# Deformable convolution and attention on one core: hand-placed order tables per engine, and token turns moved to the row-sum banks

## The reference

```python
x = x + deform_conv(group_norm(x))        # 3x3 taps, each with its own learned shift, bilinear
t = tokens(x)                             # 8 x 1024 x 64
t = t + attention(ln(t))                  # one head of 64, causal, 1024 queries and keys
t = t + experts(ln(t))                    # 32 experts, each takes its 8 best tokens per image
```

## Time and profile before

| | us |
|---|---|
| median of three executions | 601.82 (600.0 to 602.16) |
| the profiled execution | 599.73 |
| its span, first to last instruction | 597.9 |
| busy in the span: PE, PEld, DVE, ACT, POOL | 471.5, 322.1, 307.3, 277.9, 142.2 |
| mean granted clock of TensorE, as a share of 2.4 GHz | 0.852 |

### The profile page before, as it was taken

One profiled execution on the slowest core, in us unless ns is written; L12 is line 12 of the kernel. 1 busy time (PEld: TensorE's weight loads), 2 busy tenths in 40 slices (PEclk: granted clock), 3 DMA queues, 4 the chain that ended last, 5 costly groups with the idle time before them and its releaser, 6 DMA issues. The chain is left out here.

```text
span 597.9 us, 13359 instructions
## 1 busy us (share of the span) xinstructions
PE 471.5 (79%) x5651; PEld 322.1 (54%) x5651; DVE 307.3 (51%) x446; ACT 277.9 (46%) x457; POOL 142.2 (24%) x113
## 2 busy tenths in 40 slices
PE   2407877899899988998899889989988967825585
PEld 1105654656565665665566566655755643423364
DVE  3225656486647564756674657465655444223023
ACT  1223633575456555655666266636645523502210
POOL 4400034034023411342152305230223123031000
PEclk9957868999979988998999689969998965875577
DMA  9589697687356636654584458346540000005606
GB/s 235 103 184 218 165 224 190 141 197 180 85 139 161 156 90 159 156 133 124 148 208 106 99 123 210 99 123 164 139 100 2 1 0 1 1 2 114 203 2 141
DMA packets 31953, 75.10 MB, mean 126 GB/s; under 512 B 21581, under 2 KB 23437, under 8 KB 25549
## 3 DMA queue, kind: packets, MB, share of 16 engines
q1 hardware_dynamic: 27006, 72.16, 51.2%
q10 hardware_dynamic: 4880, 2.01, 1.3%
HBM read 65.04 MB, written 7.01 MB: 121 GB/s over the span
## 5 line engine op out<-in xcount | busy, mean ns | idle before, releaser
L701 DVE TENSOR_TENSOR wring<-stage 96x640 f32<-96x640 f32 x192 | 157.9, 851 | 110.8 <-ACT stage L560 104.3
L874 PE MATMUL psum<-wring,zring 96*64 96x160 f32 (+4 forms) x1728 | 150.8, 312 | 19.2 <-ACT wA L1147 17.1
L874 PEld LDWEIGHTS psum<-wring,zring 96*64 96x64 f32 x1728 | 118.7, 154 | 52.2 <-issue 33.1
L567 ACT ACTIVATE zring<-psum 96x768 f32<-96x768 f32 x64 | 51.5, 805 | 91.8 <-PE psum L841 91.8
L745 PE MATMUL psum<-keys,asked 64*128 64x128 f32 (+3 forms) x240 | 58.3, 522 | 27.0 <-DVE asked L663 16.2
L667 DVE TENSOR_REDUCE negmax<-psum 128x1 f32<-128x256 f32 (+3 forms) x64 | 52.6, 821 | 49.6 <-PE psum L751 49.0
L586 ACT ACTIVATE pT<-psum 128x512 f32<-128x512 f32 (+2 forms) x96 | 46.8, 488 | 67.3 <-PE psum L762 66.5
L841 PE MATMUL psum<-kern,img 64*32 64x192 f32 x1536 | 65.0, 373 | 9.4 <-ACT zring L567 4.1
L762 PE MATMUL psum<-const,prob 128*128 128x128 f32 x288 | 52.5, 294 | 8.5 <-ACT pT L586 6.2
L605 ACT ACTIVATE prob<-psum,negmax 128x256 f32<-128x256 f32 (+3 forms) x64 | 50.4, 788 | 10.3 <-DVE negmax L667 10.1
L254 POOL TENSOR_SCALAR gs<-gs 64x1 f32<-64x1 f32 x8 | 9.1, 1139 | 167.9 <-DVE gs L246 167.9
(11 more groups left out here) (120 smaller groups left out, 507.6 us busy)
## 6 DMA issues: line engine op xcount, KB each, us to landing
stage<-near SPq DMA_DIRECT2D x192, 288.0 KB, 4.9
w<-in_w SPq DMA_DIRECT2D x1, 2080.0 KB
tok<-in_x SPq DMA_DIRECT2D x8, 256.0 KB, 5.9
img<-img SPq DMA_DIRECT2D x8, 256.0 KB, 3.1
images<-img SPq DMA_DIRECT2D x8, 256.0 KB, 3.7
w<-in_w SPq DMA_DIRECT2D x1, 2048.0 KB
near<-tents SPq DMA_DIRECT2D x32, 45.0 KB
shifts<-offT SPq DMA_DIRECT2D x8, 128.0 KB, 5.0
```

The lines of the kernel that those rows point to most:

```text
L567: act.activation(zring[0:KX, q % ZRING].rearrange("p (s e) f -> p e s f", e=2), psum[0:KX, 0:2, 0:2 * K * C].rearrange("p e (s f) -> p e s ...
L701: dve.tensor_tensor(rows[:, ky, :, place], stage[0:KX, q % STG, ky, 1:, :], stage[0:KX, q % STG, ky, 0, :].unsqueeze(1).to_broadcast([KX, ...
L874: ins = pe.matmul(psum[C * e:C * e + C, 2 + half, (lo % 16) * W:(lo % 16 + n) * W], zring[0:KX, q % ZRING, i % 2 * 2 + e, ky * C:(ky + 1) ...
```

## The change

- The common grid of 36 steps goes. Each engine has its own table of places: `PE_TURN` (65 places), `ACT_TURN` (56), `DVE_TURN` (49); places above a table's length fall into the next turn. The helpers `stands` and `which` look a place up; `turn_tables` picks the table.
- Turns go from b = 0 to 8 instead of 9. In the last one image 7 follows the `_LAST` tables and what is left of image 6 the `_LATE` tables.
- Pairs stand two by two in places, and the masks are written as a step of their own ahead of the scores (`pe_mask`, start=True), the scores adding to them.
- Tokens, projections, tokens2 and logits use banks 0 and 1 in place of 4 and 5. All users of banks 0 and 1 wait through `take_shared` for the last user's evacuation. The scores no longer wait for the logits.
- Image 7's odd score blocks use banks 2 and 3, its odd chunks bank 1.
- The sum into the tokens (x2) is a step of its own, at the place behind share.

The arithmetic is the same. The rest of the diff replaces step numbers by table look-ups.

```diff
@@ the tables (their _LAST and _LATE forms are cut to PE's and DVE's) @@
-        AT_X, AT_RAW, AT_STATS, AT_GROUPS, AT_SCALES = 25, 26, 28, 30, 31
-        AT_OFF, AT_LEAVE, AT_DISTANCES, AT_TENT = 7, 8, 9, 10
-        AT_VALUES = [AT_PROBS[t + 1] + 3 + t // 4 for t in range(0, NT, 2)]
-        AT_OUT = AT_VALUES[-1] + 1
-        AT_SUM2, AT_SQUARES2 = AT_OUT + 3, AT_OUT + 5
-        AT_LN2, LOGITS_AFTER = NU + AT_SCORES[2] + 3, 2
+        PE_TURN = dict(
+            n=65,
+            pair=[8, 10, 14, 16, 23, 24, 26, 28, 33, 34, 38, 43, 49, 50, 56, 57],
+            z=[1, 12, 22, 29, 44, 48, 55, 61],
+            back=3,
+            lift=51,
+            groups=64,
+            offsets=17,
+            tokens=20,
+            query=25,
+            mask=[19, 30, 35, 41, 46, 53, 60, 70],
+            scores=[27, 31, 36, 42, 47, 54, 62, 71],
+            turned=[32, 40, 45, 52, 59, 63, 67, 69, 72, 76, 78, 80],
+            values=[58, 65, 74, 83],
+            out=86,
+            tokens2=102,
+            logits=104,)
+        PE_LAST = dict(
+            n=52,
+            back=2,
+            tokens=13,
+            query=14,
+            mask=[15, 16, 19, 23, 26, 31, 34, 38],
+            scores=[17, 18, 21, 24, 27, 32, 35, 39],
+            turned=[20, 28, 29, 33, 36, 37, 40, 41, 43, 44, 45, 46],
+            values=[30, 42, 47, 48],
+            out=49,
+            tokens2=50,
+            logits=51,)
+        PE_LATE = dict(
+            n=52,
+            mask=[-1, -1, -1, -1, -1, -1, -1, 3],
+            scores=[-1, -1, -1, -1, -1, -1, -1, 5],
+            turned=[-1, -1, -1, -1, -1, -1, 1, 4, 6, 7, 9, 10],
+            values=[-1, 0, 8, 11],
+            out=12,
+            tokens2=22,
+            logits=25,)
+        ACT_TURN = dict(
+            n=56,
+            z=[5, 13, 22, 32, 39, 42, 49, 52],
+            abs=[8, 15, 18, 24, 29, 45, 50, 53],
+            relu=[9, 16, 21, 28, 34, 47, 54, 55],
+            half=40,
+            rest=1,
+            raw=44,
+            leave=17,
+            tent=[23, 26],
+            keys=20,
+            query=25,
+            exp=[27, 30, 35, 38, 43, 48, 58, 66],
+            turned=[31, 37, 41, 46, 51, 56, 59, 60, 63, 67, 68, 70],
+            values=75,
+            keys2=89,
+            logits=92,
+            choice=6,)
...
+        DVE_TURN = dict(
+            n=49,
+            weights=[0, 5, 6, 7, 9, 11, 12, 13, 14, 19, 21, 24, 26, 27, 28, 31, 32, 33, 39, 40, 41, 45, 46, 47],
+            x1=2,
+            raw=35,
+            stats=37,
+            scales=42,
+            distances=15,
+            sum=3,
+            squares=8,
+            query=20,
+            max=[22, 25, 29, 30, 34, 36, 44, 53],
+            share=65,
+            x2=66,
+            sum2=67,
+            squares2=72,
+            choice=[1, 10, 38, 92, 97],)
+        DVE_LAST = dict(
+            n=26,
+            x1=2,
+            sum=3,
+            squares=4,
+            query=11,
+            max=[12, 14, 15, 16, 18, 19, 20, 21],
+            share=22,
+            x2=23,
+            sum2=24,
+            squares2=25,
+            choice=[0, 5, 6, 13, 17],)
+        DVE_LATE = dict(
+            n=26,
+            max=[-1, -1, -1, -1, -1, -1, -1, 1],
+            share=7,
+            x2=8,
+            sum2=9,
+            squares2=10,)
@@ banks @@
-            return 0 if alone(a) and t % 2 else 4
+            return 2 if alone(a) and t % 2 else 4
-            return 3 if alone(a) and n % 2 else 6
+            return 1 if alone(a) and n % 2 else 6
-                    ins = pe.matmul(psum[:, 4 + h, :], wA[C * h:C * h + C, :], keys[C * h:C * h + C, :],
+                    ins = pe.matmul(psum[:, h, :], wA[C * h:C * h + C, :], keys[C * h:C * h + C, :],
@@ who used banks 0 and 1 last @@
+        def take_shared(pe, user, i):
+            last, j = shared
+            if last == "z":
+                pe.wait_ge(f["z_sb"], j + 1)
+            if last == "lift":
+                pe.wait_ge(prep.s["raw_lo"], j + 1)
+                pe.wait_ge(prep.s["raw_hi"], j + 1)
...
+            if last == "query":
+                pe.wait_ge(s["q_sb"], ONE + j + 1)
+                pe.wait_ge(s["k_sb"], ONE + j + 1)
+            if last == "tokens2":
+                pe.wait_ge(s["lnT2"], ONE + j + 1)
+            if last == "logits":
+                pe.wait_ge(s["lg_sb"], ONE + j + 1)
+            shared[:] = [user, i]
@@ masks ahead of scores @@
+        def pe_mask(pe, a, t):
+            pe.wait_ge(s["ex"], ONE + a * NT + (max(t - 1, 0) if alone(a) else t))
+            if t == 1 and alone(a):
+                pe.wait_ge(s["x1"], ONE + a + 1)
+            bank, i, odd = score_bank(t, a), t // 2, t % 2
+            query = slice(i * P, (i + 1) * P)
+            if not odd:
+                pe.matmul(psum[:, bank + 1, query], exact[:, 0, :], exact[:, 2, :], start=True, stop=(t == 0),
+                          skip_group_check=True)
+            pe.matmul(psum[:, bank + odd, query], exact[:, 0, :], exact[:, 1, :], start=True, stop=False,
+                      skip_group_check=True)
-            if t == (LAST_AFTER_LOGITS if alone(a) else AFTER_LOGITS):
-                pe.wait_ge(s["lg_sb"], ONE + a)
@@ turns @@
-                for b in range(B + 2):
+                for b in range(B + 1):
                     pe_turn(pe, b)
```

More of the change, by code:

```diff
@@ new lines, in convolve_and_attend @@
+        ACT_LAST = dict(
+            n=39,
+            rest=0,
+            keys=12,
+            query=13,
+            exp=[14, 15, 18, 21, 23, 25, 28, 31],
+            turned=[17, 20, 22, 24, 26, 27, 29, 30, 32, 33, 34, 35],
+            values=36,
+            keys2=37,
+            logits=38,
+            choice=5,)
+        ACT_LATE = dict(
+            n=39,
+            exp=[-1, -1, -1, -1, -1, -1, 2, 7],
+            turned=[-1, -1, -1, -1, -1, 1, 3, 4, 6, 8, 9, 10],
+            values=11,
+            keys2=16,
+            logits=19,)
@@ new lines, in convolve_and_attend, with turn_tables @@
+        DVE_LAST = dict(
[17 more added lines that the diff above has]
+            squares2=10,)
+        def turn_tables(turn, last, late, b):
+            if b < B:
+                return turn, turn, turn["n"]
+            return last, late, 0
@@ L461, in mix_piece, with stands, which @@
+        def stands(at, name, n):
+            return at.get(name, -1) == n
+        def which(at, name, n):
+            return at[name].index(n) if n in at.get(name, ()) else None
         def mix_piece(pe, m, bank, done):
@@ L488, in alive @@
             return not isinstance(b, int) or 0 <= b < B
[L490 to L507, removed]
-            return None
         def logit_place(a):
@@ L637, in act_turn @@
                         prep.keep_raw(act, b + 2, 0)
-                    if n == AT_LEAVE and alive(b + 1):
+                    if stands(at, "leave", n) and alive(b + 1):
                         prep.leave(act, b + 1)
-                    for step in range(2):
-                        if n == AT_TENT + step and alive(b + 1):
-                            prep.tent(act, b + 1, step)
-                attention_steps(act, act_attention, b, n)
-                if b == B and n == AT_CHOICE[0] + 1:
+                    if which(at, "tent", n) is not None and alive(b + 1):
+                        prep.tent(act, b + 1, which(at, "tent", n))
@@ new lines, in pe_turn @@
+                    if which(at, "pair", n) is not None:
+                        conv_pair(pe, b, which(at, "pair", n), touched)
+                    g = which(at, "z", n)
+                    if g is not None and PIECES * b + g + 2 < NG4:
+                        take_shared(pe, "z", PIECES * b + g + 2)
+                        mix_rows(pe, PIECES * b + g + 2)
+                    if stands(at, "lift", n) and alive(b + 2):
+                        take_shared(pe, "lift", b + 2)
+                        prep.to_channels(pe, b + 2)
@@ new lines, in pe_turn @@
+                    if stands(at, "groups", n) and alive(b + 2):
+                        take_shared(pe, "groups", b + 2)
+                        prep.group_sums(pe, b + 2)
+                    if stands(at, "offsets", n) and alive(b + 1):
+                        take_shared(pe, "offsets", b + 1)
+                        prep.offsets(pe, b + 1)
+                    if stands(at, "offsets", n) and b == B - 1:
+                        take_shared(pe, "largest", 0)
+                        prep.largest_in_row(pe)
@@ L928, in fast_path_over @@
+                if stands(at, "back", n) and alive(b - 1):
+                    conv_back(pe, b - 1)
+                if alive(b - 2):
+                    pe_attention(pe, b - 2, n + past, late)
+                if alive(b - 1):
+                    pe_attention(pe, b - 1, n, at)
         def fast_path_over(eng):
```

240 lines of the change are left out of this document (105 added, 135 removed).

## The result

The changed kernel takes 534.26 us (median of 4, 530.36 to 535.99) beside 601.9 us (median of 4, 600.0 to 602.16) for the kernel before on the same chip: a ratio of 0.8873, 95% interval 0.8821 to 0.8925. Faster, as forecast, by 68 us where 56 were predicted; 534 lies in the range of 522 to 578.

The account below looks back on a forecast made before the run. It took TensorE (PE) to bound the kernel; full turns -40.7, turn 7 -5.8, turn 1 -2.4 and last images -7.0 sum to -55.9 us: 543.8 profiled, 546 as median, range 522 to 578, chance 0.65.

Parts of the forecast that it names:

- The bound: Five full turns: TensorE (PE) bounds; its work at full clock is 47.2 us a turn, less 0.4, of 57.4.
- the wait for asked: First scores waiting for DVE's copy of the projected queries: 16.2 us in 8 times, to fall under 5.
- The stall and its second price: First scores: the 2.57 us wait goes, and with it the slow clock following it, which costs as much as all idling.
- Rival A: Full turns: stall goes, clock falls all the same from other waits or thin products; turn 53.5, 571 us; chance 0.15.
- Idle and clock of the full turns: Full turns: 1.5 us idle and 1.0 for the clock a turn, making 49.3 us; five turns -40.7 us.
- Modes side by side: PE's tile-mode changes fall from 401 to 367 at 0.10 us each: 0.4 us a full turn, 3.4 in all.
- Rival D: Whole kernel: the change does only what its words say, products side by side; 3.4 us, 598 us; chance 0.04.
- Banks: Scores' 6.5 us of waits for logits go; handovers of banks 0 and 1 are covered, with 29 us of 48 used.
- Rival C: Banks 0 and 1 become the bound, 1.0 us a handover; full turn 61.5 us, about 625 us; chance 0.07.
- Turn 1, turn 7, turn 0: Short turns: turn 1 45.8 us (-2.4), turn 7 43.6 us (-5.8), turn 0 held by loads, 39.7 us (0).
- Last images: Up to the end of out: earlier first scores -2.2 us, own table -4.8, together -7.0, from 0 to -15.
- DMA share: Full turns: DMA's share rises from 0.58 to 0.68, short of the 0.89 of the first turn.

Follow-up runs that it names:

- experiment 2: Changed kernel with the Relu of the third piece behind both tents (ACT place 27 instead of 21): 594.51 us, ratio 1.0008.
- experiment 3: Changed kernel with the third piece's Relu at ACT's place 26: 570.27 us; or with DVE's copy of the queries at place 22 instead of 20: 547.57 us.
- experiment 7: Changed kernel with the squares of image 6's second LN later on DVE: place 12, 534.66 us; place 15 with a choice step moved too, 534.06 us.
- experiment 5: Changed kernel with the masks back behind the scores of their block: 538.42 us, ratio 0.9019.
- experiment 4: Changed kernel with tokens, projections and logits of the full turns back in banks 4 and 5, with the waits this needs: 566.07 us, ratio 0.9462.
- experiment 1: Kernel before with DVE's copy of the projected queries one step earlier: 603.45 us, ratio 1.0185.
- experiment 9: Kernel before with the copy of the queries one step earlier and share, sum into the tokens and second LN's sums 2 to 4 later: 609.64 us, ratio 1.0229.

## Why the prediction was right, and where it was off

**The bound.** Right: PE's work at the full clock bounds the full turns. The prediction had 46.8 us for it, and 47.4 was measured. The turns of 47.6 us on average lie below the 48 to 50 that it named as its sign, for the reasons below; its other signs came (clock 1.00 in them, the wait for asked at 3.8 us, low stretches only outside them).

**The stall and its second price.** Right, and the largest part. "The slow clock follows the stall" was the main assumption; experiments 2 and 3 show it. At one place, with all else equal:

| idle ahead of the first scores, us | full turn, us | low clock behind it, us |
|---|---|---|
| 0 (changed kernel) | 47.7 | 0 |
| 1.18 | 48.9 | 0 in the profiled execution |
| 1.82 | 49.5 to 56.2 | 0 to 17.1 |
| 2.78 | 57.9 | 17.1 |

The order of time foreseen around the scores came out step by step, at 4.6 us for 5.0. Rival A, that the clock falls for another reason, falls for the full turns: with the stall gone the clock holds, and with the stall alone put back it drops. In the last images experiment 7 shows a low stretch that no single long wait precedes.

**Idle and clock of the full turns.** This term of the sum was mis-sized. "I take 1.5" of idling was 0.16 on average (0.8 us in five turns), the 1.0 for "a clock that now and then still falls" was nothing, and work was 0.6 more. Together 47.6 for 49.3, so -49.3 instead of -40.7 us. The price of idling isn't smooth, and the estimate treated it as if it were: it put a middling idle time beside a middling clock loss. By the table, a stall of 1.2 us brought none of the low clock in the profiled execution, the same 1.82 us between none and 17.1 us of it, and 2.8 us the 17.1 in every full turn. Once every cover holds, both terms go to zero together.

The work came out 0.6 more because the prediction took off too much for the clock: it counted half the length of every low stretch as lost. Turns of one kernel that idle alike show less. In experiment 3 the turn with 3.4 us of low clock is 1.4 us longer than the one with none (50.9 for 49.5), and that with 13.7 us is 6.0 longer (55.5). In experiment 2 a turn is 10.2 us longer than in the changed kernel; 2.65 of it is more idling, which leaves 7.6 for 17.1 us. That is 0.41 to 0.44 of the length, and an estimate at 0.44 for the kernel before (some 51.7 us of low clock in its full turns) gives a loss of 22.7 us for the 25.8, or 0.6 more work a turn.

**Modes side by side.** Right in size as far as it was tried: 0.4 us a turn was priced for four changes, and experiment 5 has 0.43 for two of them and some idling. The Trainium skill, "TensorEngine Tiling (Array Packing)", section "Key Properties", says that a change of tiling mode drains TensorE; by that sentence the change costs something, and the 0.10 us a time of the earlier trace rows is what it is here. Rival D, that this is all the change does, falls: it is some 3 of 68 us by estimate (34 changes of 0.10), and experiment 2 loses nearly the whole gain with every one of these changes still saved.

**Banks.** The cover that the prediction counted (29 of 48 us) was enough, and PE loses nothing in take_shared. That the move is needed was underestimated. The prediction booked it as 6.5 us of waits for logits gone; experiment 4 puts it at some 30 us in this order of places, most of it by the clock, as in the new order the token turn would wait 1.9 us for banks 4 and 5. Rival C, a wait of 1 us a handover, doesn't appear: ACT is busy 163.9 of 237.9 us and follows. "PSUM Bottleneck" of the same page of the Trainium skill, which spoke for it, isn't borne out here either after the change. (The arithmetic of two rivals is off by 0.2: five turns of 53.5 us are -19.7 and five of 61.5 are +20.3. Nothing hangs on it.)

The parts aren't a sum. Without the Relu's place 60 us are lost, without the banks some 30, and the gain was 68. Each fault alone brings a stall or two, and one of 2.8 us a turn is enough for the low clock in every full turn; in the kernel before, mending one of several brought nothing (experiments 1 and 9). That was not in the prediction, which priced the old kernel's stall as if it could be taken out alone.

**Turn 1, turn 7, turn 0.** 46.3, 43.3 and 39.5 us for 45.8, 43.6 and 39.7. Right in size; in turn 1 two errors cancel. The wait for the first image's LN was kept at the 3.44 us of the earlier trace rows and fell to 1.16, and the clock was lower than assumed (0.86; 0.93 before). A low stretch of 10.2 us that lay at 76.3 to 86.5 us in the kernel before, in turn 0, now lies at 86.6 to 96.8, almost all of it in turn 1. It begins within the 3.64 us for which the turn back at 87.73 waits. Turn 0, at clock 0.89 instead of 0.78, takes 39.5 us for 39.7.

**Last images.** Mis-sized: -11.0 for -7.0 us, inside the bounds of 0 to -15. The squares waiting for POOL ahead of the copy came as foreseen. The scores started 19.6 us after the turn back, where the prediction had 19.0 (21.2 before). What it missed lies behind them: 24.2 us to the end of out, forecast 28.7, before 33.8. There PE idles 2.2 us, forecast 5, and at clock 0.86 the same working gives a clock loss of 3.4, forecast 5.5, as the clock is low for 6.8 us only. The own tables are 4.9 us of the 11.0.

**DMA share.** 0.68 was forecast for the full turns and 0.75 came, for two reasons: the turns got shorter still, and a piece takes longer to land (5.6 us, had 4.9). It never stands ahead of PE in the full turns.

## What to carry to other kernels

Where a stall of two to three microseconds stands ahead of every low stretch of TensorE's clock, price it with that stretch: here 2.8 us of idling a turn cost 10.2. Such a gain doesn't come in parts that add up, since the stall moves to the next late step when one instruction is moved, so lay out for each engine what stands between two products and check every cover before building. And look afterwards not at the sum of the edits but at which single place, put back, brings the stall again.

## What the runs showed of the hardware that was not expected

POOL got slower, with the same instructions. In the earlier trace rows the product of 64x1024 took 3784 ns and that of 128x512 1041 ns; in the changed kernel:

```profile
L258 POOL TENSOR_SCALAR img<-img,gs 64x1024 f32<-64x1024 f32 x8 | 44.1, 5513 | 0.9
L1338 POOL TENSOR_TENSOR norm_tmp<-tok,rn_small 128x512 f32<-128x512 f32 x8 | 11.2, 1397 | 66.4 <-DVE rn_small L1319 66.4
```

The traces show what goes with it. First the product in a full turn of the changed kernel, then the same one in experiment 2, where DVE stands idle beside it because its weights product waits for the late Relu:

```profile
202.23 1.52 POOL L1338 TENSOR_TENSOR norm_tmp<-tok,rn_small 128x512 f32<-128x512 f32 x1 [6.25 <-DVE rn_small L1319]
```

```profile
166.77 1.04 POOL L1338 TENSOR_TENSOR norm_tmp<-tok,rn_small 128x512 f32<-128x512 f32 x1 [6.25 <-DVE rn_small L1319]
```

With a weights product of DVE beside it (202.02, 0.82 us) it takes 1.52 us, with none 1.04, and so it is in each of the five full turns of both kernels. It goes the other way too: in experiment 1 POOL's product starts at 163.27 and takes its 1.04 us, and DVE's weights product, started at 163.34, takes 1.65 us for 0.82. That fits what the Trainium skill, "GPSIMD Engine Reference", section "Specifications", says, that the two engines contend when DVE reads two inputs from SBUF. So POOL's time depends on which of DVE's products fall beside its own, and DVE is now busy 181.7 of 237.9 us in the full turns (174.5 of 287.2 before). It costs nothing there, as PE doesn't wait for POOL in the full turns; in the last images, where PE does, the product takes 1.04 us.

The same idle time doesn't bring the same low stretch: after 1.82 us at the same place of five equal turns it lasted 0, 3.4, 3.4, 13.7 and 17.1 us. And executions of the same kernel differ by up to 7 us (529.4 to 536.12), while the full turns of its two profiled ones agree to 0.1 us a turn.
